# Edge products of a two-layer graph and mixture-of-experts kernel: one factor through PSUM, and zero rows written chunk by chunk

## The reference, cut to what matters

```python
# layer 0: graph step, A = adj [5000, 5000], 0 or 1
adj0 = A * (y @ y.T)
row_l1 = max(sum(abs(adj0), axis=1), 1e-12)
x = x + 0.9 * (adj0 / row_l1) @ layernorm(x) + 0.1 * h0
# layer 0: shared expert, and 2 of 8 routed experts per row (hidden width 512)
x = x + shared(xn) + sum over the top two e of weight_e * expert_e(xn)
# layer 1: graph step; the edge term is what the change touches
n = layernorm(x)
edge = einsum('ij,ji->i', A, A)[:, None]
x = x + concat(n, A @ n, edge) @ weight + bias
# layer 1: 2 of 8 routed experts per row (hidden width 256)
```

## Time and profile before

| | |
|---|---|
| median of three runs | 1938.49 us (1930.33 to 1942.17) |
| the profiled execution's own time | 1940.99 us |
| its span | 1939.2 us |
| mean granted TensorE clock | 0.862 |
| busy over the span: PE, DVE, POOL, ACT | 1403.7, 1306.6, 1008.4, 638.0 us |
| first loop: start to the copy that ends chunk 9 (line 863) | 0 to 1039 us |
| routed experts of layer 0, then the second loop, to about | 1340 us, 1700 us |

### The profile page before, as it was taken

The page is one execution under the profiler, slowest core; times in us unless marked ns, Lnnn a source line. Parts: engine busy times, 40 slices in busy tenths (PEclk is TensorE's granted clock), DMA queues, the critical chain, the costliest instruction groups (busy, mean ns, idle before and its releaser), DMA issues. The chain is left out here.

```text
span 1939.2 us, 23686 instructions
## 1 busy us (share of the span) xinstructions
PE 1403.7 (72%) x5510; PEld 882.1 (45%) x5510; DVE 1306.6 (67%) x3129; ACT 638.0 (33%) x1048; POOL 1008.4 (52%) x820
## 2 busy tenths in 40 slices
PE   4565677767676766767676799976999999836762
PEld 1232333333243333333334587862666666636662
DVE  6536598989899898979896222228777777733324
ACT  2213333223232232323222244431555555412321
POOL 4423566656656565656554254552355555546663
PEclk9777788979888787878887799998999999958876
DMA  9985679776767676767765355527888988624544
GB/s 315 390 301 150 243 284 310 275 288 256 285 241 290 233 293 251 268 248 277 270 246 225 133 178 168 178 90 260 285 303 295 308 304 294 209 80 143 154 143 176
DMA packets 132323, 467.32 MB, mean 241 GB/s; under 512 B 21759, under 2 KB 34082, under 8 KB 96258
## 3 DMA queue, kind: packets, MB, share of 16 engines
q1 hardware_dynamic: 90064, 405.42, 59.0%
q10 hardware_dynamic: 29330, 37.07, 5.8%
q0 software_dynamic: 12832, 23.81, 3.5%
HBM read 411.93 MB, written 59.51 MB: 243 GB/s over the span
## 5 line engine op out<-in xcount | busy, mean ns | idle before, releaser
L323 POOL TENSOR_TENSOR absum<-mabs,absum 128x512 f32<-128x512 f32 x330 | 458.9, 1391 | 380.6 <-ACT mabs L877 321.0
L621 PE MATMUL agg<-m,xn 128*128 128x512 f32 x800 | 483.6, 691 | 36.8 <-DVE m L1237 36.8
L605 PE MATMUL s<-ymov,ysta 128*128 (+1 forms) x400 | 270.9, 681 | 304.2 <-DVE m L1237 284.4
L877 ACT ACTIVATE mabs<-m 128x512 f32<-128x512 f32 x390 | 243.7, 630 | 627.6 <-DVE m L1237 399.6
L1237 DVE TENSOR_TENSOR m<-s,ring 128x512 f32<-128x512 f32 x400 | 272.5, 684 | 83.6 <-issue 39.8
L605 PEld LDWEIGHTS s<-ymov,ysta 128*128 128x128 f32 x400 | 88.3, 221 | 528.0 <-DVE m L1237 468.5
L1260 DVE CUSTOM_DVE_ANT_0 junk<-ring 128x512 bf16<-128x512 f32 x320 | 320.0, 1002 | 12.3 <-DMA ring<-in_adj_out 12.1
L1472 POOL DMA_INDIRECT y_scratch<-yo,ids x216 | 213.0, 986 | 209.1 <-DVE yo L1151 131.0
L1463 POOL DMA_INDIRECT rows_scratch<-xrow,idx x160 | 199.8, 1249 | 122.3 <-issue 65.8
L621 PEld LDWEIGHTS agg<-m,xn 128*128 128x128 f32 x800 | 176.0, 222 | 109.2 <-DVE m L1237 50.8
L678 PE MATMUL d<-wb,h 128*128 128x128 f32 x1296 | 178.0, 291 | 41.2 <-ACT h L905 41.2
(11 more groups left out here) (189 smaller groups left out, 1940.6 us busy)
## 6 DMA issues: line engine op xcount, KB each, us to landing
ring<-in_adj_in SPq DMA_DIRECT2D x200, 1024.0 KB, 5.1
ring<-in_adj_out SPq DMA_DIRECT2D x80, 1024.0 KB
wb<-blob_scratch SPq DMA_DIRECT2D x27, 834.0 KB
rows_scratch<-yo ACTq DMA_DIRECT2D x81, 260.0 KB, 7.8
ring<-in_adj_in SPq DMA_DIRECT2D x80, 256.0 KB
ring<-in_adj_out SPq DMA_DIRECT2D x80, 256.0 KB
xt<-rows_scratch SPq DMA_DIRECT2D x54, 260.0 KB
wb<-blob_scratch SPq DMA_DIRECT2D x27, 449.0 KB
```

The lines of the kernel that those rows point to most:

```text
L323: eng.tensor_tensor(absum[:], mabs[:, b % 2, :], absum[:], ALU.add).then_inc(abs_added, 1)
L605: pe.matmul(sbank[s % 2][:], ysta[:, s * P:(s + 1) * P], ymov[:, k % 2, :], start=True, stop=True).then_inc(s_made, 1)
L621: pe.matmul(abank[:], xn[:, b, :], m[:, b % M_BUFS, :], start=b == 0, stop=b == NB - 1).then_inc(S["agg_blocks"], 1)
L877: act.activation(mabs[:, b % 2, :] if b else absum[:], m[:, b % M_BUFS, :], ACT.Abs).then_inc(abs_made, 1)
```

## The change

First, the edge products of the first loop get one factor from PSUM. ScalarE copies each outgoing block (and each outgoing late block) to one of two PSUM banks in turn, `ubank[1]` and `dbank[1]`. The order of the 50 operations of a chunk is the list `EDGE_ORDER`. A copy waits until the product two places before it in that order is done (`wait_edge_bank`); a product waits for its copy (`edge_copied`). ACT, no longer DVE, waits for the outgoing loads. SP waits for the copies before it loads outgoing slots again.

Second, the shared expert uses `ubank[0]` alone, so its next first product waits for the gelu of the one before.

Third, the zero rows are written chunk by chunk. In each of the ten chunks ACT starts one transfer of 260 KB in steps 6, 10, 14 and so on, eight a chunk and nine in chunk 0, for the regions' rows of that chunk alone. POOL's waits before the scatter follow.

```diff
+EDGE_ORDER = [op for s in range(1, NB + 1)
+              for op in ([("late", s // LB)] if s % LB == 2 and s < NB else []) + [("own", s - 1)]]
...
+    ebank = [ubank[1], dbank[1]]
...
+    def wait_edge_bank(eng, k, kind, i):
+
+        n = EDGE_ORDER.index((kind, i)) - 2
+        chunk, (old, b) = (k - DEFER if n >= 0 else k - DEFER - 1), EDGE_ORDER[n % len(EDGE_ORDER)]
+        if old == "own":
+            wait(eng, edges_read, chunk * NB + b + 1)
+        else:
+            wait(eng, late_read, chunk * XPER + b + 1)
...
             if isinstance(k, int) and l < 2:
                 sp.wait_ge(m_made, (k * LOADS + l - 1) * LB)
+            else:
+                last = ((l - 2) % LOADS + 1) * LB - 1
+                wait(sp, edge_copied, edge_number(k if l >= 2 else k - 1, "own", last) + 1)
+                carry(sp, sp_carried)
...
-            wait(pe, ffn_gelu, j * HID[0] + hb - 1)
-            at, u = slice(hb * P, (hb + 1) * P), ubank[hb % 2]
+            wait(pe, ffn_gelu, j * HID[0] + hb)
+            at, u = slice(hb * P, (hb + 1) * P), ubank[0]
...
+        def copy_edge(k, kind, i, src):
+
+            wait_edge_bank(act, k, kind, i)
+            act.copy(ebank[EDGE_ORDER.index((kind, i)) % 2][:], src).then_inc(edge_copied, 1)
...
-                    if s >= 8 and s % 3 == 2 and (s - 8) // 3 <= CH:
-                        null_rows((s - 8) // 3)
...
+                if agg and s >= 6 and s % 4 == 2 and (s - 6) // 4 <= (E if isinstance(k, int) and k == 0 else E - 1):
+                    null_rows(k, (s - 6) // 4)
...
+                if agg and not (isinstance(k, int) and k < DEFER):
+                    if s % LB == 2 and s < NB:
+                        i = s // LB
+                        wait(act, late_landed[i % 2], 32 * ((k - DEFER) * (XPER // 2) + i // 2 + 1))
+                        copy_edge(k, "late", i, late[:, i % 2, 1, :])
+                    if 1 <= s <= NB:
+                        l, at = (s - 1) // LB, (s - 1) % LB * CW
+                        if (s - 1) % LB == 0:
+                            wait(act, ring_landed[2 + l % 2], in_count(k, l))
+                        copy_edge(k, "own", s - 1, ring[:, 2 + l % 2, at:at + CW])
                 if agg and 1 <= s <= NB:
...
-                    dve.tensor_tensor_reduce(late[:, i % 2, 0, :], late[:, i % 2, 0, :], late[:, i % 2, 1, :],
+                    dve.tensor_tensor_reduce(late[:, i % 2, 0, :], edge_bank(("late", i)), late[:, i % 2, 0, :],
...
-                    if b % LB == 0:
-                        wait(dve, ring_landed[2 + l % 2], in_count(k, l))
+                    wait(dve, edge_copied, edge_number(k, "own", b) + 1)
...
-                    dve.tensor_tensor_reduce(junk[:, b % 2, :], ring[:, l % 2, piece], ring[:, 2 + l % 2, piece],
+                    dve.tensor_tensor_reduce(junk[:, b % 2, :], edge_bank(("own", b)), ring[:, l % 2, piece],
```

More of the change, by code:

```diff
@@ L401, in late_loads @@
             wait(sp, late_read, (k - DEFER) * XPER + i - 1)
+            carry(sp, sp_carried)
+            wait(sp, edge_copied, edge_number(k, "late", i - 2) + 1 if i >= 2 else
+                 edge_number(k - 1, "late", XPER + i - 2) + 1)
             carry(sp, sp_carried)
@@ L664, in tile_up_part @@
             wait(pe, tile_gelu, n - 1)
+            if n == 1:
+                pe.wait_ge(edges_read, (CH - DEFER) * NB)
             pe.matmul(u[:], tile_part(t, "high", hb), xnfh[:], start=True, stop=False)
@@ L673, in tile_down_part @@
                 pe.wait_ge(ffn_added, CH)
+            if t == 1 and hb == 0:
+                pe.wait_ge(late_read, (CH - DEFER) * XPER)
             if hb == 0:
@@ L1457, in scatter_rows @@
                 wait(pool, weights_made, g + 1)
-                if isinstance(g, int) and g < 2:
-                    pool.wait_ge(rows_nulled[g], 16 * E)
-                elif isinstance(g, int):
-                    pool.wait_ge(rows_nulled[2], 16 * (E * (CH - 2) + 1))
+                if layer == 0 and isinstance(g, int) and g < 2:
+                    pool.wait_ge(rows_nulled[g], 16 * (1 + E if g == 0 else E))
+                elif layer == 0:
+                    wait(pool, rows_nulled[2], 16 * E * (g - 1))
                 carry(pool, pool_carried)
@@ L1494, in a_iteration @@
                 if mid and A_AT["scatter"] <= s < A_AT["scatter"] + 2 * TB:
-                    scatter_rows(k - 1, s - A_AT["scatter"])
+                    scatter_rows(0, k - 1, s - A_AT["scatter"])
         a_pipeline(pool, a_iteration)
```

35 lines of the change are left out of this document (22 added, 13 removed).

## The result

| | before | after |
|---|---|---|
| median of four runs each | 1935.1 us (1930.3 to 1942.2) | 1864.5 us (1861.5 to 1866.6) |
| ratio, 95% interval | | 0.963 [0.959, 0.967] |
| profiled span | 1939.2 us | 1865.0 us |
| chunk 0 | 116.6 us | 88.5 us |
| chunk 1 | 112.6 us | 114.7 us |

A chunk is counted here from the start of the copy of the chunk sum (`aggf`) that ends one chunk to the start of the next one's. The span fell by 74 us: 28 in chunk 0, less 2 in chunk 1, 45 in chunks 2 to 9, 3 behind the loop. The forecast was 1851 us: 28, less 2, and 62.

The account below looks back on a forecast made before the run. VectorE was taken to bound the eight chunks with edge products. 62 us there plus 28 in chunk 0 less 2 in chunk 1, off 1941.0, gives 1853; the median, 2.5 lower, 1851 us (range 1832 to 1868; 8 in 10: 1800 to 1893).

Parts of the forecast that it names:

- What comes back: Chunks 2 to 9: of 15.5 us a chunk of removed product waiting, 7.8 return as other waits, leaving 7.7.
- Light rounds: Two short load rounds a chunk stop at 7.6 us, 3.0 MB at 393 GB/s, giving back 0.9 and 1.9 us.
- Hand-off: Where an outgoing load is late, its landing releases a copy, then the product; 0.8 us a chunk given back.
- The round from 594.0: A load round of chunk 5, starting at 594.0 us: stays at 7.8 us, just above the 7.6 us transfer floor.
- Zero rows: Chunk 0 gains 28 us, chunk 1 loses 2; in chunks 2 to 9 one 0.27 MB transfer is counted in the rounds.
- Scatter and last round: Chunk ends: two rounds with POOL's scatter keep their length, 1.4 us not gained; last round 8.5 us, 2.8 back.
- The transfers' ceiling: Load rounds: the sum used the measured 393 GB/s, 7.6 us a round, against the skill's 358, which gives 8.4.
- Transfers keep up: Rival, chunks 2 to 9: only the scatter gives back, 14.1 us a chunk gained, about 1800 us; chance 0.15.
- Transfers cap earlier: Rival, load rounds: 361 GB/s, 8.3 us for 3.0 MB, 5.1 us a chunk gained, 1872 us; chance 0.14.
- ScalarE paces the loop, weakly: Rival, ScalarE's queue: copies and absolute values queue behind each other, 3 us a chunk gained, 1889 us; chance 0.06.
- The slower case: Rival, ScalarE's in-order queue: copies behind absolute values waiting for POOL, 16 us more a chunk, 2041 us; chance 0.05.
- doesn't do what it says: Rival, edge products: from PSUM they still take 1002 ns, only chunk 0 gains, 1913 us; chance 0.05.

Follow-up runs that it names:

- copy_unused: The changed kernel with ScalarE's copies and their waits kept, but VectorE's edge products reading both factors from SBUF; 1877.9 us, ratio 0.993.
- split_late: The changed kernel with each 1 MB load issued as two halves and the late pair of loads ahead of the outgoing second half; 1769.8 us, ratio 0.936.
- no_copy: The changed kernel without ScalarE's copies; products read stale PSUM banks and VectorE waits for outgoing loads itself; 1797.8 us, ratio 0.953.
- psum_only: The changed kernel with the zero rows written as in the kernel before, keeping copies and PSUM factors; 1838.5 us, ratio 0.974.
- split_before: The kernel before the change, with its loads split and ordered as in split_late; 1880.8 us, ratio 0.994.

## Why the prediction was right, and where it was off

- **The products.** Right: 15.5 us a chunk of waiting to go, at 687 ns; measured 683, which is 124.9 us over all 400 (320.0 + 78.0 us before, 273.1 after). The rule of the Trainium skill, page "SBUF — State Buffer", section "Who interferes with whom", held: products with one SBUF input show no spread beside GpSimd's additions, and `copy_unused` shows that this input is the reason.
- **Chunk 0.** Right: 28 us forecast, 28.1 measured; VectorE's waits for absolute values went, as did 18.8 of its 23.9 us ahead of additions. That the two agree to 0.1 us is luck, since chunk 0 scatters by 5 us from profile to profile. Chunk 1: 2 forecast, 2.2 measured.
- **What comes back.** This is the step that failed in size: 7.8 us a chunk forecast, 15.5 - 5.6 = 9.9 measured, 17 us over eight chunks, against 13.5 us between forecast and result. A chunk gave 5.6 us, less than the 6.5 to 9 from which the range was made. That the whole stayed inside the range (1832 to 1868) is in part luck: 3 of the 17 us came back behind the first loop, of which the forecast says nothing. Five places in it:
  - *Light rounds.* Forecast to stop at 7.6 us, for 3.0 MB over 393 GB/s. They are 7.0 and 7.1 us: that floor isn't there, since a round's bytes needn't move within the round. In the case above 2.4 MB moved in the light round and 3.4 in the one behind it. A load lands 7.4 us after its issue even so, and the price is paid in the round behind: the third is 11.2 us, longer than the 10.3 before, and had no term in the sum. `split_late` has 5.8 and 6.0 us in the light rounds and 10.0 in the third, with all bytes.
  - *Hand-off.* Forecast 0.8, measured 3.4 by `no_copy`. The forecast took the copy's length at three late loads. It had no term for the first round of a chunk (17.4 us with copies, 15.9 without, and never below 17.1 in any of the tabulated kernels that copy). There the copy waits on ScalarE behind the gelu, some 1.4 us a chunk, whatever the load does: one of the prediction's own signs of being wrong, VectorE idle behind a copy whose load has landed.
  - *The round from 594.0,* the seventh. Forecast 7.8 us; it is 8.7 to 9.1 in all kernels with a PSUM factor. Two errors met here. First, the x8 in the earlier trace rows counts four products and four reads of the accumulator, 0.08 us each, so 0.33 us too much was called waiting; the same 0.33 us stands in the light rounds and the last one. Second, other instructions of VectorE began to wait for GpSimd, as the last section shows.
  - *Zero rows.* In chunks 2 to 9 they were put inside the light rounds. `psum_only` puts them at 1.7 us a chunk.
  - *Scatter and last round.* These came right: the eighth and ninth together are 16.1 us before and after, and the last is 8.7 where 8.5 was forecast.
- **The transfers' ceiling.** The forecast kept to the measured 393 GB/s over the 358 of the Trainium skill, page "DMA: Bandwidth & Descriptors", section "Where 436 GB/s comes from". The trace goes above both in a short stretch: 402 GB/s for 5.8 us at the loop's turn of the changed kernel. No run tests how long such a rate can be held in the chunks: `split_late` moves 334 GB/s in the mean, 363 in the nine rounds above.
- **ScalarE.** Forecast 66 us busy with issues; its recorded work is 442.4 / 8 = 55.3 us a chunk, 50 x 0.585 = 29 of it copies. Its order mattered, as the gelu ahead of a copy shows; whether its length did, no run tests alone.
- **The rivals.** "Transfers keep up" (1800 us) describes the kernel once its loads are split: the bytes fit, if only just. "Transfers cap earlier" (1872 us) is nearer in time than the forecast (7.5 us off against 13.5), but its light rounds of 8.3 us did not come. "ScalarE paces the loop, weakly" (1889 us) named a wait that is there, copies behind other work in the queue, at some 1.4 us a chunk; VectorE gained 5.6 us a chunk and not 3. The slower case (117 us a chunk) fell with the chunks' 95.6 us, and "doesn't do what it says" with the product's 683 ns.

## What to carry to other kernels

- When a change speeds up the bound engine, ask of each transfer how long it takes from issue to landing and how long the work is that covers it. The bytes of one round over a rate gave a floor that wasn't there, since the queue carries them into the next round, and hid the wait that was.
- A late load costs less if it is issued in the order and the size in which its parts are used: two edits on SP's queue took 7.1 us of 95.4 from each chunk, with no byte less. Without a bound that has moved to the transfers (`split_before`), they give 0.6%.
- A copy on another engine's in-order queue lengthens the wait when its input is late, and takes over the waits of whatever stands ahead of it when its input is early (here the gelu). The two should be measured together and apart, since their costs don't add, and by rounds, since a small net can hide two large differences.
